# Shorter router chain and a rearranged gather stage in a two-layer graph transformer

## What is computed

```python
x = x + switch_ffn(layernorm(x))     # layer 0
xn = layernorm(x)
h = relu(concat(xn, agg) @ W1 + b1)  # layer 1; agg: mean edge features per node, (1024, 64)
x = x + (xn + h @ W2 + b2) + splat_attention(xn)

def switch_ffn(xf):
    logits = xf @ switch_w.T + switch_b          # (1024, 16)
    probs = softmax(logits); route_probs = max(probs); routes = argmax(probs)
    oh = one_hot(routes); pos = cumsum(oh, axis=0)[token, routes] - 1
    keep = pos < capacity                        # capacity 76
    buf = zeros(E, capacity, D).at[routes, pos].set(xf)
    y = einsum('ecd,efd->ecf', buf, expert_w) + expert_b
    gathered = y[routes, minimum(pos, capacity - 1)]
    return where(keep, gathered, xf) * route_probs
```

## Time and profile before

| | us |
|---|---|
| three runs, median | 861.49 |
| lowest, highest | 861.15, 863.32 |
| profiled execution: time | 859.79 |
| profiled execution: span, first to last instruction | 858.0 |

### The profile page before, as it was taken

One profiled execution on the slowest core, in us unless ns is written; L12 is line 12 of the kernel. 1 busy time (PEld: TensorE's weight loads), 2 busy tenths in 40 slices (PEclk: granted clock), 3 DMA queues, 4 the chain that ended last, 5 costly groups with the idle time before them and its releaser, 6 DMA issues. The chain is left out here.

```text
span 858.0 us, 11649 instructions
## 1 busy us (share of the span) xinstructions
PE 775.5 (90%) x4058; PEld 572.3 (67%) x4058; DVE 616.8 (72%) x1225; ACT 381.5 (44%) x583; POOL 117.2 (14%) x91
## 2 busy tenths in 40 slices
PE   4989999999999982699599999899989999999998
PEld 3777887888778861465287777665556566665876
DVE  7777887776758757698864424288986888898646
ACT  2342343343214412375321202855632888887453
POOL 3000000000000005010454000444340013000000
PEclk9999999999999995699589999999999999999999
DMA  5563322310302142999320301100000000010002
GB/s 183 155 204 114 100 74 58 89 41 8 123 0 99 50 176 98 264 377 317 108 99 1 99 0 50 50 0 2 1 2 3 3 1 1 1 56 2 1 1 98
DMA packets 48152, 66.63 MB, mean 78 GB/s; under 512 B 4268, under 2 KB 22460, under 8 KB 48095
## 3 DMA queue, kind: packets, MB, share of 16 engines
q1 hardware_dynamic: 43903, 56.22, 20.3%
q0 software_dynamic: 2384, 6.92, 2.5%
q10 hardware_dynamic: 1808, 2.75, 0.9%
HBM read 56.38 MB, written 9.50 MB: 77 GB/s over the span
## 5 line engine op out<-in xcount | busy, mean ns | idle before, releaser
L974 PE MATMUL bank<-xT,slot 128*128 128x512 f32 (+1 forms) x248 | 107.2, 432 | 2.7 <-DVE xT L1782 2.3
L975 PE MATMUL bank<-xT,slot 128*128 128x512 f32 (+1 forms) x248 | 99.0, 399 | 0.0
L976 PE MATMUL bank<-xT,slot 128*128 128x512 f32 (+1 forms) x248 | 98.5, 397 | 0.0
L1485 ACT ACTIVATE slot<-bank 128x512 fp32r<-128x512 f32 (+3 forms) x60 | 34.2, 586 | 137.7 <-PE bank L1241 56.3
L974 PE MATMUL bank<-slot 128*128 128x512 f32 (+1 forms) x212 | 83.2, 392 | 5.2 <-DVE slot L1782 1.9
L974 PE MATMUL bank<-slot,xT 128*128 128x512 f32 (+1 forms) x192 | 78.7, 410 | 2.8 <-DVE slot L2296 1.9
L976 PE MATMUL bank<-slot 128*128 128x512 f32 (+1 forms) x212 | 80.8, 381 | 0.0
L975 PE MATMUL bank<-slot 128*128 128x512 f32 (+1 forms) x212 | 80.8, 381 | 0.0
L2321 DVE TENSOR_REDUCE key<-bank 128x2 f32<-128x1024 f32 x64 | 74.3, 1218 | 6.9 <-PE bank L1301 6.9
L976 PE MATMUL bank<-slot,xT 128*128 128x512 f32 (+1 forms) x192 | 76.1, 396 | 0.0
L975 PE MATMUL bank<-slot,xT 128*128 128x512 f32 (+1 forms) x192 | 75.9, 395 | 0.0
(11 more groups left out here) (339 smaller groups left out, 1637.3 us busy)
## 6 DMA issues: line engine op xcount, KB each, us to landing
arena<-in_ewT SPq DMA_DIRECT2D x16, 1024.0 KB, 11.1
arena<-in_edge_attr SPq DMA_DIRECT2D x16, 512.0 KB, 3.9
wraw<-in_qkvT SPq DMA_DIRECT2D x3, 1024.0 KB, 5.1
...
wraw<-in_L_mix_w_qkv SPq DMA_DIRECT2D x2, 1024.0 KB, 8.1
```

What stands on the lines that cost most here:

```text
L974: pe.matmul(out, L[1], R[0], start=start, stop=False, **kw)
L975: pe.matmul(out, L[0], R[0], start=False, stop=False, **kw)
L976: return pe.matmul(out, L[0], R[1], start=False, stop=stop, **kw)
L1485: act.activation(h, src, kw.pop("func", ACT.Copy), **kw).then_inc(hi_done, 1)
```

## The change

The router's bias is added by ScalarE as it evicts the logits (per partition, since experts lie on partitions there), and the maximum is taken from PSUM. The one-hot is bf16; the running totals come from TensorE, which adds ones-products over the earlier tiles to the triangle's product in one bank (tot0 falls away; GpSimd makes bf16 copies of both matrices early in the kernel). The index is formed in five operations; the gather's index, and the kept flag, follow after route_ready. Tile 7 is normalised before the low parts of tiles 4 to 6, and the logits of the second half are computed for tiles 4 to 6 first, then for tile 7. Bias rows 0 and 2 are loaded before the scatters.

In the gather stage the aggregates' transposes stand between the transposes of expert 15 and the products of expert 14; ScalarE evicts them before its last two sends, with the high part of W1a between these two; GpSimd writes the row of ones. The aggregates' part of W1 is loaded when expert 14's weight is split. VectorE splits W2a only after the low parts of tiles 0 to 3, forms tile 4's residual before the second normalisation, and does the splat parameters in HW(0,0)'s step. The diff, cut:

```diff
@@ -151,18 +151,19 @@
-            add(*step, bank={("lT", 0, 0): 6, ("rt0", 0): 7, ("cum0", 0): 6, ("tot0", 0): 7,
-                             ("lT", 0, 1): 4, ("rt0", 1): 0, ("cum0", 1): 1, ("tot0", 1): 2}[step])
+            add(*step, bank={("lT", 0, 0): 6, ("rt0", 0): 7, ("cum0", 0): 6,
+                             ("lT", 0, 1): 4, ("rt0", 1): 0, ("cum0", 1): 1}[step])
...
+        if e == EXPERTS - 1:
+            for g in range(2):
+                add("aggT", g, bank=2 + g)
...
+    for t in range(TH):
+        add("xT", 2, t, bank=4 + t)
...
-    add("aggT", 0)
-    add("aggT", 1)
-    for t in range(TH):
-        add("xT", 2, t)
@@ -850,7 +854,7 @@
-            finished(sp, "eY", EXPERTS - 1)
+            sp.wait_ge(ew_split, 2 * (EXPERTS - 1))
@@ -888,18 +892,31 @@
+            pool.wait_ge(all_taken, 1)
+            pool.tensor_copy(tri16_first, tri).then_inc(counts_ready, 1)
+            pool.tensor_copy(ones16, ones).then_inc(counts_ready, 1)
...
+            pool.wait_ge(w_split, windex["Wv"] + 1)
+            def load_bias(e):
+                pool.dma_start(eb[e % 4], a["L0_ffn_expert_b"][e:e + 1].to_broadcast([CAPR, D])).then_inc(eb_in[e % 4], 16)
+            load_bias(0)
+            load_bias(2)
...
-            for e in range(EXPERTS):
-                if e >= 4:
-                    emptied(pool, "eY", e - 4)
-                pool.dma_start(eb[e % 4], a["L0_ffn_expert_b"][e:e + 1].to_broadcast([CAPR, D])).then_inc(eb_in[e % 4], 16)
+            load_bias(1)
+            load_bias(3)
+            for e in range(4, EXPERTS):
+                emptied(pool, "eY", e - 4)
+                load_bias(e)
+            pool.wait_ge(ew_split, 2 * (EXPERTS - 1))
+            pool.memset(aggT[EA:EA + 1, :], 1.0).then_inc(blk_ready, 1)
@@ -1189,11 +1206,13 @@
-                    for t in range(th * TH, (th + 1) * TH):
-                        emptied(pe, "xT", 1, t)
...
-                    for k in range(C):
-                        ins = mm3(o[0:EXPERTS, :], hl(swP, k), hl(xT[th], k), k == 0, k == C - 1)
+                    for lo_, hi_ in (((0, TH),), ((0, TH - 1), (TH - 1, TH)))[th]:
+                        for t in range(lo_, hi_):
+                            emptied(pe, "xT", 1, th * TH + t)
+                        w = slice(lo_ * P, hi_ * P)
+                        for k in range(C):
+                            ins = mm3(o[0:EXPERTS, w], hl(swP, k), hl(xT[th], k, w), k == 0, k == C - 1)
@@ -1205,10 +1224,22 @@
+                    pe.wait_ge(counts_ready, 2)
+                    o = open_bank(*step)
+                    def tiles(first, last):
+                        return chosen16[:, first * EXPERTS:last * EXPERTS]
+                    if th:
+                        for d in range(TH, T):
+                            pe.matmul(o[:, (d - TH) * EXPERTS:TH * EXPERTS], ones16, tiles(0, T - d), start=d == TH, stop=False)
...
-                    chosen = tail[:, 2, th * TH:(th + 1) * TH, :].rearrange("p t e -> p (t e)")
-                    o = open_bank(*step)
-                    close(pe.matmul(o[:, 0:TH * EXPERTS], tri if step[0] == "cum0" else ones, chosen, start=True, stop=True))
+                    pe.matmul(o[:, 0:TH * EXPERTS], tri16_first, tiles(th * TH, (th + 1) * TH), start=th == 0, stop=False)
+                    for d in range(1, TH):
+                        lo_ = 0 if th else d
+                        ins = pe.matmul(o[:, lo_ * EXPERTS:TH * EXPERTS], ones16, tiles(th * TH + lo_ - d, (th + 1) * TH - d),
+                                        start=False, stop=d == TH - 1)
+                    close(ins)
@@ -1219,6 +1250,12 @@
+                if e == EXPERTS - 1:
+                    for g in range(2):
+                        o = open_bank("aggT", g)
+                        for j in range(4):
+                            ins = pe.transpose(o[0:EA, chunk(j)], agg[:, 4 * g + j, :], ident)
+                        close(ins)
@@ -1229,12 +1266,6 @@
-            for g in range(2):
-                o = open_bank("aggT", g)
-                for j in range(4):
-                    ins = pe.transpose(o[0:EA, chunk(j)], agg[:, 4 * g + j, :], ident)
-                close(ins)
@@ -1577,7 +1608,8 @@
-                act.activation(lT[0][:, th * HALF:(th + 1) * HALF], at("lT", 0, th)[0:EXPERTS, :], ACT.Copy).then_inc(evicted[bank_of[("lT", 0, th)]], 1)
+                act.activation(lT[0][:, th * HALF:(th + 1) * HALF], at("lT", 0, th)[0:EXPERTS, :], ACT.Identity,
+                               bias=switch_bias).then_inc(evicted[bank_of[("lT", 0, th)]], 1)
@@ -1595,7 +1627,7 @@
-                    if step[2] == T - 2:
+                    if step[2] == TH:
@@ -1627,14 +1659,18 @@
+            act.wait_ge(ew_split, 2 * (EXPERTS - 1))
+            for g in range(2):
+                finished(act, "aggT", g)
+                act.activation(aggT[0:EA, g * HALF:(g + 1) * HALF], at("aggT", g)[0:EA, :], ACT.Copy).then_inc(evicted[bank_of[("aggT", g)]], 1)
...
+            split_weight("W1a")
...
-            split_weight("W1a")
...
-                for t in range(2 * g, 2 * g + 2):
-                    hi(("xT", 2, t))
+            for t in range(TH):
+                hi(("xT", 2, t))
@@ -2072,46 +2110,31 @@
-                dve.tensor_tensor(L[:, w], by_tile(name), sbrow[:, :].unsqueeze(1).to_broadcast([P, TH, EXPERTS]),
-                                  ALU.add).then_inc(evicted[bank_of[name]], 1)
-                emptied(dve, *name)
-                link(dve.tensor_reduce(c_a[:, w], L[:, w], AX, ALU.max))
-                ins = dve.tensor_tensor(X[:, w], L[:, w], over_e(c_a[:, w], EXPERTS), ALU.subtract)
-                if th:
-                    ins.then_inc(logit_ready, 1)
-                link(dve.tensor_tensor(OH[:, w], L[:, w], over_e(c_a[:, w], EXPERTS), ALU.is_equal))
+                link(dve.tensor_reduce(c_a[:, w], by_tile(name), AX, ALU.max))
+                link(dve.tensor_tensor(OH[:, w], by_tile(name), over_e(c_a[:, w], EXPERTS), ALU.is_equal))
...
-                dve.tensor_tensor(OH[:, w], Y[:, w], over_e(c_b[:, w], EXPERTS), ALU.is_equal).then_inc(onehot_ready, 1)
+                dve.tensor_tensor(chosen[:, w], Y[:, w], over_e(c_b[:, w], EXPERTS), ALU.is_equal).then_inc(onehot_ready, 1)
+                ins = dve.tensor_tensor(X[:, w], by_tile(name), over_e(c_a[:, w], EXPERTS), ALU.subtract)
+                ins.then_inc(evicted[bank_of[name]], 1)
+                emptied(dve, *name)
+                if th:
+                    dve.sem_inc(logit_ready, 1)
+                link(dve.tensor_scalar(c_e[:, w], c_b[:, w], -float(CAPR), float(SLOTS), ALU.mult, ALU.add))
+                link(dve.tensor_tensor(c_h[:, w], c_e[:, w], kst[:, K_TOK + th * TH:K_TOK + (th + 1) * TH], ALU.subtract))
...
-                tot, cum = ("tot0", th), ("cum0", th)
+                cum = ("cum0", th)
...
-                finished(dve, *tot)
...
-                if th == 0:
-                    link(dve.memset(Z[:, 0, :], 0.0))
-                last = TH if th == 0 else T - 1
-                for t in range(th * TH + 1, last + 1):
-                    ins = dve.tensor_tensor(Z[:, t, :], by_tile(tot)[:, t - 1 - th * TH, :], Z[:, t - 1, :], ALU.add)
-                    if t < last:
-                        link(ins)
-                ins.then_inc(evicted[bank_of[tot]], 1)
-                emptied(dve, *tot)
-                dve.tensor_tensor(Z[:, w], by_tile(cum), Z[:, w], ALU.add).then_inc(evicted[bank_of[cum]], 1)
+                dve.tensor_tensor(Z, by_tile(cum), chosen[:, w], ALU.mult).then_inc(evicted[bank_of[cum]], 1)
...
-                link(dve.tensor_tensor(Z[:, w], Z[:, w], OH[:, w], ALU.mult))
-                link(dve.tensor_reduce(c_d[:, w], Z[:, w], AX, ALU.add))
-                link(dve.tensor_scalar(c_e[:, w], c_b[:, w], -float(CAPR), float(SLOTS), ALU.mult, ALU.add))
-                link(dve.tensor_scalar(c_f[:, w], c_d[:, w], float(CAP), None, ALU.is_lt))
-                link(dve.tensor_scalar(c_g[:, w], c_d[:, w], float(CAP - 1), None, ALU.min))
-                link(dve.tensor_tensor(c_g[:, w], c_g[:, w], c_e[:, w], ALU.add))
-                link(dve.tensor_scalar(c_h[:, w], c_f[:, w], -1.0, 1.0, ALU.mult, ALU.add))
-                link(dve.tensor_tensor(c_d[:, w], c_g[:, w], c_f[:, w], ALU.mult))
-                link(dve.tensor_tensor(c_e[:, w], kst[:, K_TOK + th * TH:K_TOK + (th + 1) * TH], c_h[:, w], ALU.mult))
-                dve.tensor_tensor(idx[:, 0, w], c_d[:, w], c_e[:, w], ALU.add).then_inc(route_ready, 1)
+                link(dve.tensor_reduce(c_d[:, w], Z, AX, ALU.add))
+                link(dve.tensor_tensor(c_g[:, w], c_d[:, w], c_h[:, w], ALU.add))
+                link(dve.scalar_tensor_tensor(c_f[:, w], c_d[:, w], float(CAP), c_g[:, w], ALU.is_lt, ALU.mult))
+                dve.tensor_tensor(idx[:, 0, w], c_f[:, w], kst[:, K_TOK + th * TH:K_TOK + (th + 1) * TH], ALU.add).then_inc(route_ready, 1)
@@ -2131,20 +2154,22 @@
```

(32 more changed lines are left out.)

47 lines of the change are left out of this document (26 added, 21 removed).

## The result

The changed kernel takes **849.4 us**, median of four runs (848.38 to 853.34), beside 861.9 for the kernel before on the same chip: ratio 0.9857, 95% interval 0.9835 to 0.988. Two further sets of runs gave 0.9854 (0.9833 to 0.9875) and 0.9866 (0.9844 to 0.9887). The forecast was 855.5 with a range of 852.0 to 859.2. The profiled execution took 849.56 us, its span is 847.0 (before 858.0), its mean granted clock 0.968 (before 0.960).

A forecast was written before the change was run, and what follows sets the result against it. TensorE was taken as busy nearly everywhere except two holes, router and gather, where chains bound it; 4.3 + 1.7 = 6.0 us saved, set against the median 861.49, gave 855.5 us, range 852.0 to 859.2.

The forecast's parts named there:

- Hole A: Router stretch, about 330 to 350 us, TensorE partly idle: shorter chain to the second half's index, 4.3 us saved in sum.
- step 1: Router: tile 7 normalised before the splits, last products in two column groups; 1.8 us saved, bounds 1.5 and 3.9.
- the counts: Router: two fp32 count products become four bf16 ones, some run before the one-hot; 1.27 us to 0.95, 0.3 us saved.
- Never falls: Router's last products: TensorE's clock stays full throughout, the upper bound of 3.9 us saved by order and column groups.
- more than forecast: Rival: router's products at full clock, earlier last write, or earlier clock rise in experts or gather stage; 852 us, chance 0.12.
- 14.6 us that the change leaves as they are: From the fifth scatter's start to the experts' start: 14.6 us, taken as unchanged.
- scatters become the bound: Rival, router: all three later scatters meet splits and take 1.96 us, the stretch grows 1 to 2; 857.5 us, chance 0.14.
- Step 5: Gather stage: aggregates' transposes stand before the last but one expert product, so the last expert product ends 0.75 us later.
- Step 6: Gather stage: last write takes 3.55 us instead of 4.1; gathers from 410.2 last 1.0 us each, second lands at 415.0.
- The gather gives nothing: Rival, gather stage: W1a lands late and its copy delays the last send and all gathers; 857.2 us, chance 0.08.
- Step 7: Gather stage: VectorE is the chain from the second gather's landing; first product with W1 at 427.9 instead of 429.66.
- The clock in H: Rival, W1 products: TensorE idles beforehand, so half clock lasts longer; slower, up to 871.9 us, chance 0.04 beyond break-even.

The follow-up runs named there:

- e14: Kernel before, nothing of the change, with 12 unread products ahead of tile 7's transposes and 5 ahead of the router's second half: 861.05 us, ratio 0.9975.
- e13: Changed kernel with 6 unread products ahead of tile 7's transposes and 5 ahead of the router's second half: 848.7 us, ratio 0.9843.
- e1: Kernel before with only the router part of the change (order, groups, pick, counts, index, biases): 853.41 us, ratio 0.9893.
- e4: Changed kernel with VectorE's expert splits, and residual updates behind them, held until all scatters landed: 853.12 us without one 3621 us execution, ratio 0.9895.
- e9: Changed kernel with VectorE's split of W2a put back before the residual updates, beside the gathers: 853.59 us, ratio 0.9886.
- e12: Changed kernel with bias loads 1 and 3 held until the first row load landed, plus unread products before experts and around first gathered transposes: 847.04 us, ratio 0.982.
- e6: Changed kernel with all four bias loads put back behind the scatters: 853.45 us, ratio 0.9885.
- e2: Kernel before with only the gather part of the change, the router as before: 859.49 us, ratio 0.9968.
- e3: Changed kernel with tile 7's root and normalisation put back behind the splits of tiles 4 to 6: 851.97 us, ratio 0.9888.

## Why the prediction was wrong

The forecast for the span was 852.0; it is 847.0. By the table, the 5.0 us are: 2.7 at S5 (forecast 330.5, found 327.79), 2.1 in S5-E, 1.2 in E-X, 0.1 in X-G, 0.4 from there to H, less 1.6 lost behind H. Of the 2.7 at S5, 0.4 lie upstream of the change.

- **Hole A's sum of 4.3 us was nearly right at full clock on both sides.** There (e14 and e13) tile 7's residual to S5 takes 16.30 and 12.33 us: 3.97. For the changed kernel the forecast, 330.5, stands 14.66 us behind that residual; the four profiles at half clock have 14.62 or 14.63, e1, whose clock rose as I had assumed, 13.72. So the agreement of 4.35 (before, rising, against changed, half) with 4.3 is in part luck: with a rising clock on both sides it is 5.26. The parts at full clock: step 1 gave 1.70 for 1.8, the pick 0.39 (1.64 to 1.25) for 0.35, the index 1.89 (2.96 to 1.07) for 1.85, the counts 0.11 for 0.3. The counts' old row, 1.12 us, stood at half clock, and most of what the two profiles show between them, 1.27 to 0.70, is again the clock. The trace of before had the same four records at full clock, for the first half's counts (0.56 us from 316.88), and I passed them over.
- **The step that failed first is the clock in step 1.** I let it rise where it had risen before. It was full from the first product in the changed kernel's profiles, worth 2.3 us (14.63 against 12.33). The edits don't fix it: with the changed router it was full in nine profiles (two of them with products to help) and half or rising in six, and of these e4, e9 and e12 run the changed kernel's own code up to there, e6 all of it but two bias loads. Whether the edits make the full clock more frequent is not shown: without help the old router was rising in both of its profiles (before, e2), and the changed kernel itself was full in all three. "Never falls" was my bound of 3.9 us for step 1, and the chance of the case "more than forecast", 0.12, was too small for something of which I had only one trace.
- **"14.6 us that the change leaves as they are" was wrong by 2.1 us, and by more against e2 and e14, which needed 16.4 and 16.0.** I had written down that two bias loads leave the stretch behind the scatters, and gave them no price. They shared the way with the row load: 2.7 us (e6 against e1). And the overlap of scatters and splits did not stay: the phase went from 6.80 to 5.84 us, since the splits began 1.5 us behind the fifth scatter, not 0.7. My own times, 331.7 and 330.5, already put 1.2 us between them. In the first pair of profiles the phase is 1.0 of the 2.1 us and the load (6.0 to 4.9) 1.1; by the means of before, e2 and e14 (15.67) and of the changed kernel's three profiles (12.11) the segment gives 3.6 us, which makes it the largest error of the forecast. The rival "scatters become the bound" went the other way; it came true only in e3, where GpSimd's queue set S5.
- **Step 5** charged 0.75 us to the experts' end for the aggregates' transposes. E-X was 55.25 to 55.86 in the changed kernel, 55.27 and 55.74 in the code before: no charge to be seen, though the clock rose after 10 slow products there instead of 13, worth about 0.6 us at 0.2 us each, which may hide it.
- **Step 6** put the last write at 3.55 us. X-G, which contains it, was 4.8 to 5.0 before and 3.6 to 4.3 with the changed gather stage; the forecast was 4.3. The last send's write landed 2.5 us after its issue, against 3.2 before. The margin held: W1a had landed at 393.0, and the send went out at 396.34, 0.03 us after the last bias add. ScalarE's copy of W1a ended only at 396.47, so the send does not wait for its end. "The gather gives nothing" did not occur.
- **Step 7 was right.** G-T was forecast at 10.0 us (410.2 to 420.2) and was 9.7; T-H at 7.7, and was 7.6. The W2a split beside the gathers accounts for 1.8 of the 2.5 us. The Trainium skill (SBUF — State Buffer, "Who interferes with whom") infers that such a subtraction does not block the writing of descriptors, but has it contend with a GpSimd instruction that reads SBUF. The scatters and gathers here take their index from SBUF, and the delay depends on what is under way at their start; 2.86 us in e9 and 0.97 us for all held scatters in e4 show the delay, but not which of the two steps of the DMA it holds. So "by that rule the overlap costs nothing" went further than the page does.
- **"The clock in H"** ended on the good side: ten products with W1 were slow instead of 14, and the clock was full from 421.5, 4.4 us after H's start instead of 6.2.
- **Behind H** nothing should have changed, but the profile lost 1.6 us. H-end was 427.5 to 430.7 in all kernels without unread products before H, 428.3 and 429.1 in the code before, so this is within what profiles of kernels with the same code behind H differ by; in the changed kernel's profile two stretches of the splat stage stood at 0.66 (537.5 to 542.5) and 0.91 (607.5 to 627.5). Whether the change has a part in it is not shown.
